# A routed feed-forward layer: expert rows in 25 tiles of 256 and 21 units of 128 instead of 39 tiles of 256

## The reference

```python
t = h.reshape(B * S, -1)                      # 4096 tokens x 256
logits = t @ W_gate + b_gate
probs = jax.nn.softmax(logits, axis=-1)
topv, topi = jax.lax.top_k(probs, TOP_K)      # 2 of 8 experts
topv = topv / jnp.sum(topv, axis=-1, keepdims=True)
mid = jax.nn.relu(jnp.einsum('nd,edh->neh', t, W1) + b1)    # 256 -> 1024
eout = jnp.einsum('neh,ehd->ned', mid, W2) + b2             # 1024 -> 256
moe_out = jnp.einsum('ne,ned->nd', route, eout)
out = moe_out.reshape(B, S, -1) @ W_out + b_out
```

## Time and profile before

| | |
|---|---|
| median of 3 executions | 553.31 us (551.42 to 557.58) |
| profiled execution | 553.89 us |
| its span, first to last instruction | 552.1 us |
| mean granted TensorE clock | 0.969 |
| TensorE matmuls busy | 520.3 us (94%) |
| VectorE, ScalarE, GpSimd busy | 348.9, 282.4, 221.8 us |

### The profile page before, as it was taken

One profiled execution on the slowest core, in us unless ns is written; L12 is line 12 of the kernel. 1 busy time (PEld: TensorE's weight loads), 2 busy tenths in 40 slices (PEclk: granted clock), 3 DMA queues, 4 the chain that ended last, 5 costly groups with the idle time before them and its releaser, 6 DMA issues.

```text
span 552.1 us, 13863 instructions
## 1 busy us (share of the span) xinstructions
PE 520.3 (94%) x4337; PEld 450.1 (82%) x4338; DVE 348.9 (63%) x697; ACT 282.4 (51%) x499; POOL 221.8 (40%) x286
## 2 busy tenths in 40 slices
PE   7888966999999999999999999999999999994897
PEld 6555744888888888888888888888888888883786
DVE  4669896686675675665666666675556656651564
ACT  2335782766565565565654654754334324320662
POOL 4400007146373374374375365365334334212132
PEclk8798996999999999999999999999999999998799
DMA  7405445548465364255255256222445445304973
GB/s 210 145 2 165 169 134 161 146 136 171 79 153 162 76 186 128 67 160 163 69 142 170 76 149 166 69 74 78 116 118 143 124 115 137 76 20 142 387 291 134
DMA packets 82312, 74.68 MB, mean 135 GB/s; under 512 B 47511, under 2 KB 70236, under 8 KB 82268
## 3 DMA queue, kind: packets, MB, share of 16 engines
q1 hardware_dynamic: 72336, 49.96, 32.3%
q0 software_dynamic: 8608, 24.13, 14.2%
q10 hardware_dynamic: 1324, 0.05, 0.2%
HBM read 45.53 MB, written 18.61 MB: 116 GB/s over the span
## 4 chain that ended last, share of the span: by engine, by line
PE 85%; DVE 5%; DMA 5%; issue 1%; ACT 1%; SPq 1%; POOL 0%; POOLq 0%; DVEq 0%; ACTq 0%
PE bank L1229 36%; PE bank L1199 13%; PE bank L1200 12%; PE bank L1201 12%; PE bank L1267 5%; DMA z_by_token<-w1s 2%; DVE w1s L822 2%; PE bank L1277 1%; DMA w1s<-y_by_choice 1%; PE bank L1064 1%; DMA w1s<-in_x 1%; PE bank L1215 1%; PE bank L1094 1%; PE bank L1074 1%; DMA region<-z_by_token,src 1%
## 5 line engine op out<-in xcount | busy, mean ns | idle before, releaser
L654 ACT ACTIVATE region<-bank,b1p,cbits 128x256 f32<-128x256 f32 x312 | 159.1, 560 | 183.6 <-PE bank L1201 175.9
L1229 PE MATMUL bank<-w2s,region 128*128 x1824 | 205.3, 273 | 0.1
L1229 PEld LDWEIGHTS bank<-w2s,region 128*128 128x128 f16 x1824 | 178.4, 98 | 21.0 <-issue 0.4
L1199 PE MATMUL bank<-region,w1s 128*128 128x256 f16 x624 | 171.1, 274 | 0.9 <-ACT region L641 0.9
L1200 PE MATMUL bank<-region,w1s 128*128 128x256 f16 x624 | 171.1, 274 | 0.0
L1201 PE MATMUL bank<-region,w1s 128*128 128x256 f16 x624 | 171.0, 274 | 0.0
L522 POOL DMA_INDIRECT y_by_choice<-region,dst x78 | 84.5, 1083 | 189.7 <-DVE region L971 173.2
L514 POOL DMA_INDIRECT region<-z_by_token,src x78 | 77.5, 994 | 86.2 <-DMA z_by_token<-w1s 62.6
L983 DVE TENSOR_TENSOR region<-region 128x512 f16<-128x512 f32 x156 | 108.4, 695 | 5.4
L981 DVE CAST region<-region 128x512 f16<-128x512 f32 x156 | 67.7, 434 | 66.3 <-ACT region L654 61.2
L971 DVE SCALAR_TENSOR_TENSOR region<-bank,cbits,b2b 128x256 f32<-128x256 f32 x76 | 33.3, 479 | 78.4 <-PE bank L1229 77.9
(11 more groups left out here) (239 smaller groups left out, 383.3 us busy)
## 6 DMA issues: line engine op xcount, KB each, us to landing
region<-in_L_ffn_W SPq DMA_DIRECT2D x16, 1024.0 KB, 5.2
w1s<-y_by_choice SPq DMA_DIRECT2D x13, 512.0 KB, 10.2
w1s<-in_x SPq DMA_DIRECT2D x8, 512.0 KB, 8.8
z_by_token<-w1s SPq DMA_DIRECT2D x16, 256.0 KB, 2.5
region<-in_x SPq DMA_DIRECT2D x8, 256.0 KB, 4.0
out<-region POOLq DMA_DIRECT2D x8, 256.0 KB, 5.6
region<-z_by_token,src POOLq DMA_INDIRECT x78, 2.9
y_by_choice<-region,dst POOLq DMA_INDIRECT x78
```

The source lines that it names most:

```text
L654: m = s.activation(midf[:, b, c * TS:(c + 1) * TS], FB[b][:, c * TS:(c + 1) * TS], ACT.Relu, bias=b1p[:, bass.ds(r, 1), f:f + 1].rearrange ...
L1199: mm(o, w, xs[:, par, 0, k, :], start=(k == 0), stop=False)
L1229: last = mm(YB[par][:, h * D:(h + 1) * D], mids[:, par, l, b, c * TS + h * P:c * TS + (h + 1) * P], w2_at(e, w, f), start=(f == 0 and l == ...
```

## The change

The rows are laid out anew. The first 25 tiles (NBIG) hold 256 rows each and only whole tiles of an expert; what is left of each expert goes into 21 units (NUNIT) of 128 rows. That makes 46 steps (NSTEP) on TensorE, ScalarE and VectorE: v = 0 to 24 are tiles, 25 to 45 are units. For gather, turn and scatter two units form a pair, so that there are 36 "tiles" (NTILE, 25 + 11, the last with one unit), 71 blocks of 128 rows (NA) where there were 78.

A unit's first layer (first_unit) still has 48 matmuls, with 128 moving columns, and reads W1 from w1u, one of two fixed buffers in SBUF in the place of raw1 and raw2, at addresses without a register. SP fills them by DMA from w1s (copy_w1): 1 MB per unit, 8 KB in each of 128 partitions. copy_w1(v) reads the unit's expert from tile_e into a register first, then waits until the first layer of unit v - 2 is done, since it overwrites its buffer. A unit's second layer (second_unit) has 24 matmuls of 256 columns with W2 at an address from a register, as before.

Other parts: GT is 3, so that weights are made every 3 tiles; the loop of TensorE's program holds 6 tiles and runs 3 times; VectorE computes slots for the two kinds of rows; the residual uses other buffers and is loaded during the units; 4 of the 16 add_bias follow the last y_out.

```diff
+    NBIG = -((E * (TS - 1) - K * N) // TS)
+    NUNIT = (K * N + E * (P - 1)) // P - NBIG * H
+    NSTEP = NBIG + NUNIT
-    NTILE = (K * N + E * (TS - 1)) // TS
-    NA = NTILE * H
+    NTILE = NBIG + (NUNIT + H - 1) // H
+    NA = NBIG * H + NUNIT
...
+        w1u = region[:, RR:RR + 2 * RAW].bitcast(f16).rearrange("p (s l k f) -> p s l k f", s=2, l=2, k=KD)
...
-        GT = NT * P * K // TS // E
+        GT = (NBIG - 1) // E
+        def rank_of(a):
+            return max(a - 1, 0) // GT
+        def phase(a):
+            return a - 1 if a <= GT else (a - 1) % GT
+        def first_step(a):
+            return a if a < NBIG else NBIG + (a - NBIG) * H
+        def halves(a):
+            return H if a < NTILE - 1 else NA - (NTILE - 1) * H
+        def last_step(a):
+            return first_step(a) + (0 if a < NBIG else halves(a) - 1)
+        def rows_done(a):
+            return 16 * (H * ((a + 1) // 2 - 1) + halves(a))
...
             def turn(a):
-                sp.wait_ge(s_g[a % 2], 16 * H * ((a + 1) // 2))
+                sp.wait_ge(s_g[a % 2], rows_done(a))
                 if a >= 2:
-                    sp.wait_ge(s_mp, 4 * (a - 1))
-                for h in range(H):
+                    sp.wait_ge(s_mp, 4 * (last_step(a - 2) + 1))
+                for h in range(halves(a)):
...
+            def copy_w1(v):
+                u = v - NBIG
+                e = sp.value_load(tile_e[0:1, v:v + 1], min_val=0, max_val=E - 1)
+                if u >= 2:
+                    sp.wait_ge(s_mp, 4 * (v - 1))
+                else:
+                    sp.wait_ge(s_wl, 4 * E)
+                sp.dma_start(w1u[:, u % 2].rearrange("p l k f -> p (l k f)"),
+                             w1s[:, bass.ds(e, 1)].rearrange("p e l k f -> p (e l k f)")).then_inc(s_wu[u % 2], 16)
...
             for a in range(NTILE):
                 if a + 2 < NTILE:
                     turn(a + 2)
...
+                if a == NBIG - 2:
+                    for v in range(NBIG, NBIG + 2):
+                        copy_w1(v)
+                if a >= NBIG:
+                    for v in range(first_step(a) + 2, last_step(a) + 3):
+                        if v < NSTEP:
+                            copy_w1(v)
+                if NBIG + 1 <= a < NBIG + NS // 2 - 1:
+                    load_residual(a - NBIG - 1)
...
+            link(v.scalar_tensor_tensor(small[:, 1, :], cnt[:, 5, :], 0.0, cnt[:, 3, :], ALU.max, ALU.min))
...
+            v.tensor_tensor(sv[:], sv[:], bc(cnt[:, 4, :].unsqueeze(2), [P, E, NT]), ALU.add)
...
+            link(v.tensor_tensor(over, over, bc(small[:, 5, :].unsqueeze(2), [P, E, NT]), ALU.mult))
+            link(v.tensor_tensor(sv[:], sv[:], over, ALU.add))
...
+            def first_unit(v):
+                u, par = v - NBIG, place(v)[0] % 2
+                rows = slice(place(v)[1] * P, (place(v)[1] + 1) * P)
+                pe.wait_ge(s_xd[par], rows_done(place(v)[0]))
+                pe.wait_ge(s_wu[u % 2], 16 * (u // 2 + 1))
+                for b in range(4):
+                    pe.wait_ge(s_mf, v * 4 + (b - 3))
+                    for c in range(2):
+                        o = FB[b][:, c * P:(c + 1) * P]
+                        f = slice((2 * b + c) * P, (2 * b + c + 1) * P)
+                        for k in range(KD):
+                            mm(o, w1u[:, u % 2, 0, k, f], xs[:, par, 0, k, rows], start=(k == 0), stop=False)
+                            mm(o, w1u[:, u % 2, 0, k, f], xs[:, par, 1, k, rows], start=False, stop=False)
+                            last = mm(o, w1u[:, u % 2, 1, k, f], xs[:, par, 0, k, rows], start=False,
+                                      stop=(k == KD - 1))
+                    last.then_inc(s_mp, 1)
...
+            for v in range(NBIG, NSTEP):
+                first_unit(v)
+                if v == NBIG:
+                    second_layer(v - 1, (v - 1) % 2, expert(v - 1))
+                else:
+                    second_unit(v - 1, expert(v - 1))
+            second_unit(NSTEP - 1, expert(NSTEP - 1))
```

More of the change, by code:

```diff
@@ L268, in moe_program @@
         s_wh, s_wl = sem("weights_high"), sem("weights_low")
+        s_wu = [sem(f"unit_weights_copied{i}") for i in range(2)]
         s_bsq = sem("b1_squared")
@@ L518, in scatter @@
             def scatter(a):
-                for h in range(H):
-                    pool.wait_ge(s_ys, a + 1 + h * (a == NTILE - 1))
+                for h in range(halves(a)):
+                    pool.wait_ge(s_ys, first_step(a) + 1 + (h if a >= NBIG else 0))
                     at = dst[:, a * H + h:a * H + h + 1]
@@ L536, in _ @@
                     else:
[L537 removed]
+                        pool.wait_ge(s_xd[a % 2], rows_done(a))
                     gather(a + 2)
[L539 to L540 removed]
+                if a < NBIG and phase(a) == 2 and rank_of(a) + 1 < E:
+                    table(rank_of(a) + 1)
                 if a:
@@ L657, in tile @@
                     m.then_inc(s_mf, 1)
-                if j + 1 < E:
-                    if phase(a) == 0:
+                if v < NBIG and j + 1 < E:
+                    if phase(v) == 0:
                         w1_squares(j + 1)
                         w2_squares(j + 1)
-                    if 0 < phase(a) < 3:
+                    if 0 < phase(v) < 3:
                         for i in range(2):
-                            piece(j + 1, 2 * (phase(a) - 1) + i)
-            for a in range(NTILE):
-                tile(a, a % 2, a // GT)
+                            piece(j + 1, 2 * (phase(v) - 1) + i)
+            for v in range(NSTEP):
+                step(v)
             def copy_mix(i, par):
```

189 lines of the change are left out of this document (106 added, 83 removed).

## The result

The changed kernel takes 592.62 us (median of 4, 589.16 to 594.74) beside 552.37 us for the kernel before in the same comparison (550.95 to 557.58). The ratio is 1.070, 95% interval 1.062 to 1.079: slower by 40 us. The forecast was 590.0, range 572 to 614.

A forecast was written before the change was run, and what follows sets the result against it. TensorE's matmul time and waits were taken to bound the kernel; from 553.9 us, saving -35.4, stalls +53.7, cold clock +17.1 and front +0.5 give 589.8, said as 590, with 572 to 614 for 8 in 10.

The forecast's parts named there:

- The saving: TensorE's tile stage: 14 tiles of 10.48 us go, 21 units of 5.30 come, saving 35.4 us.
- The rival of loads that bound the matmul: Units' first layer: weight loads of up to 98 ns set the narrow matmuls' spacing; 614 to 633 us, chance 0.07.
- The stalls: TensorE waits for W1 copies queued behind SP's transposes, nine times, 6.1 us each but one of 4.85: +53.7 us.
- The rival of a slower copy: W1 copy within SBUF takes longer than a load from HBM; 603 to 617 us, chance of over 605 is 0.12.
- that of a cheap copy: W1 copy lands in 3.0 us or less, so the kernel is not slower; 548 us at 2.5, chance 0.05.
- The cold clock: After each of nine stalls TensorE runs 3.9 us at half speed, losing 1.9 us each: +17.1 us.
- The bound of 2.6 for one stall: Most a stall's clock fall could cost: 2.6 us, if the whole first unit runs at 106.7 ns per matmul.
- The rival of a clock that holds: TensorE's clock stays full through the stalls; 573 us, chance 0.14.
- The front: Before the first tile: 12 more small VectorE operations, mostly absorbed by waits on ScalarE; net +0.5 us, between -0.5 and +2.
- Weights every 3 tiles: Weight changes every 3 tiles instead of 4 lose the spare tile; 2 us at most, taken as 0.
- The end: Residual loads and last 4 add_bias lie beside the wait for scatters and pair loads: 0 us.
- the waits would name the DMA: Sign: ahead of first_unit the waits name the DMA from w1s, nine times near 6 us, 50 to 55 in sum.

The follow-up runs named there:

- run 3: Changed kernel without copies: a unit's first layer reads W1 from w1s at an address from a register; 574.52 us, ratio 1.038 to the kernel before.
- run 1: Changed kernel with the copy for the next pair's first unit put ahead of the turn in SP's queue; 538.92 us, ratio 0.976 to the kernel before.
- run 8: Changed kernel with the W1 copies issued from ScalarE's queue, behind the unit's activations, instead of SP's; 549.94 us, ratio 0.987 to the kernel before.
- run 12: Repeat of run 10 (changed kernel, first copy's register read ahead of the transposes) beside the unedited changed kernel on one chip; 613.42 us, ratio 1.101.
- run 4: Changed kernel copying only W1's high half (512 KB), used in place of the low half too; 579.32 us, ratio 1.050 to the kernel before.
- run 2: Changed kernel with 40 idle matmuls of 256 columns ahead of each of the nine waits; 583.78 us, ratio 1.057 to the kernel before.
- run 11: The changed kernel, unedited, measured again in another set; 616.36 us, ratio 1.110 to the kernel before.
- run 10: Changed kernel with only the register read for a pair's first copy moved ahead of the transposes; 612.12 us, ratio 1.094 to the kernel before.
- run 9: The kernel of run 1 measured again, unedited, on another chip; 559.02 us, ratio 1.000 to the kernel before.
- run 6: Changed kernel with both units' register reads ahead of the turn, copies still behind it; 613.25 us, ratio 1.108 to the kernel before.
- run 5: Changed kernel with both copies of a pair put ahead of the turn in SP's queue; 545.57 us, ratio 0.982 to the kernel before.

## Why the prediction was right, point by point

- **The saving, -35.4: -35.5.** A unit is 5.30, its first layer 2.68, a matmul 55.6 ns for 55.8. The front's 40 ns between loads was the right row, the 98 ns of one load its length and not its spacing (loads are 98 ns long in the changed kernel too, while matmuls stand 55.6 apart). The rival of loads that bound the matmul falls, and the 81 ns of the Trainium skill ("TensorE: Matmul & The Clock Gate", "Back-to-back issue gap") do not hold for constant addresses here; with addresses from a register run 3 has 87.
- **The stalls, +53.7: +51.0**, nine, at the units named. That the place in SP's queue is the cause is shown by runs 1 and 8: the same copies elsewhere, 9.7 and 2.1 us of waiting ahead of the units. The terms: transposes 2.54 for 2.5, register read 1.01 for 1.0 (run 12 takes it away and gains 1 each), landing of the first copy 4.66 for 5.2. This term carries the miss: nine times 0.5 us less, partly given back by two longer turns (2.95 and 3.59 us). The 5.6 us of the page are the median over both copies of a pair; the first land in 4.4 to 4.7, the second, issued 1.2 us later, in 5.6 to 7.4. The rival of a slower copy falls, that of a cheap copy too: even 512 KB left 37.8 us of waits (run 4). The Trainium skill's fit ("DMA: Bandwidth & Descriptors", "Anatomy of one DMA — SWDGE (gpsimd) path") gives 4.4 us for 1 MiB, an estimate, and was nearer to the first copy's 4.66 than the load from HBM, though it was made for another issuing engine.
- **The cold clock, +17.1: +19.3**, 2.1 per stall for 1.9. The bound of 2.6 for one stall was passed three times (2.8, 2.8 and 3.0), where the clock stayed down into the second layer. Run 2 shows that it is a cost: with six of nine units at full clock the stage is 6.5 us shorter although the gaps are 4.5 longer, so 11 of the 19.3 are back. The rival of a clock that holds falls in the windows.
- **The front, +0.5: +1.6**, inside the bounds of -0.5 to +2, but partly by luck: behind the cast the changed kernel took 3.2 us more, and it reached the cast 1.6 us sooner in this execution. The waits on ScalarE did not absorb the 12 operations as thought, as far as single traces tell.
- **Weights every 3 tiles, 0: +0.7**, below the bound of 2. **The end, 0: -1.7.** The first pair loads land in 4.45 us there, for 6.27; no edit was tried on it.
- **The sum.** 589.8 for the 589.2 of the profiled execution is closer than its terms, since their misses cancel: stalls 2.7 and the end 1.7 us shorter than forecast, the cold clock 2.2, the front 1.1 and the weights 0.7 longer.
- **What the prediction did not have:** that the time from TensorE's last matmul to the turn can be more than nothing. Its stall is a chain of queue times; in the set of run 11 this link, which it took as 0, was up to 3.0 us, and the time 616, outside its range. So it was also luck in which set the kernel was first measured.
- The prediction said that the waits would name the DMA. They said "issue"; only the short waits of run 2 name it.

## What to carry to other kernels

Before a transfer is put in a queue, ask when its buffer is free, when its data is wanted, and what stands ahead of it in that queue: here TensorE had 7.9 us of work between the two, a copy needs 4.7, and the place behind a turn that waits one unit longer made it late nine times. Put the transfer on a queue that passes the point where its buffer comes free anyway (run 8), or at least ahead of the wait (run 1). Constant addresses for narrow matmuls were worth 30 ns each, but the same idea loses when its copies are late: on one chip it is 612 us with the copies behind the turn (run 10), 559 with the first ahead of it (run 9) and 550 on ScalarE's queue (run 8).

When a time to landing or a wait changes between two runs, look at which instructions the view has counted before giving it a cause: the longer landings of runs 6 and 10 were those of other copies, not of slower ones.

A gain of 2% from one chip is not yet a gain: run 1 was 0.976 there and 1.000 on another. Of all versions only run 8 (0.987) and run 5 (0.982), each on one of the slower chips, and run 1 on the first were ahead of the kernel before, none by clearly more than 2%; which is best was not settled.

## What the runs showed of the hardware

- A matmul of 128 columns with a new weight block each: 55.6 ns at the full clock, 106.7 at half (changed kernel), 85 to 90 at full clock in nineteen of 21 units with the weights at an address from a register (run 3).
- A copy of 1 MB within SBUF, issued at 384.36 in the changed kernel's profile, moves nothing until 385.5 and then runs near 380 to 390 GB/s, with the DMA share at 1.0. It is 4.5 to 5.0 us from its issue until TensorE goes on, when it is first in line (the result and runs 6, 10, 11 and 12), and 3.0 to 3.3 for 512 KB (run 4). With TensorE at work meanwhile (run 2) it was 4.6 to 6.2.
- A stop of TensorE of 4.1 to 6.6 us was followed by the half clock each time (result, run 4), one of 2.6 us was not (run 4), and of the stops between 2.2 and 3.3 us four were and one was not (runs 1 and 2). The fall can come 0.1 to 1.3 us after work has gone on (result, runs 1, 2 and 4). In the changed kernel one stop with its fall cost 1.4 to 3.0 us beyond its length.
- Two DMA transposes hold their queue for 2.5 us in most places, 3.7 to 5.7 behind two such copies (run 5).
- Equal programs on different chips: the kernel before 552 to 559 us, the changed one 593 and 616. In the profiles of three chips SP and ScalarE go on up to 3 us after TensorE's last matmul of a step, with a releaser called "remote" (runs 5 to 12); in the changed kernel's first profile SP does so after 0.07 us.
